# One matmul of every expert tile moved into the weights: b3 made part of the up weights, in a routed mixture-of-experts kernel

## What is computed

```python
x = x + conv_part(layernorm_c(x))          # attention over each image, ends in a product with Wr plus br
t = layernorm_t(x)                         # mean 0, variance 1 over the 128 channels of a token
logits = t @ Wg                            # 8 experts
top_logits, top_idx = top_k(logits, 2)     # two experts for each token
C = one_hot(top_idx) * softmax(top_logits)
h = t @ W1[e]                              # 128 -> 384
g = t @ W3[e] + b3[e]                      # 128 -> 384, with a bias
out = sum_e C[e] * (silu(h) * g) @ W2[e]   # 384 -> 128
x = x + out
```

## Time and profile before

| | |
|---|---|
| median of 3 runs | 313.33 us (312.4 to 313.88) |
| the profiled execution, its own time | 314.3 us |
| its span, first to last instruction | 312.6 us |
| TensorE matmul, busy | 257.9 us (83%) |
| VectorE, busy | 197.9 us (63%) |
| ScalarE, busy | 149.3 us (48%) |
| GpSimd, busy | 138.5 us (44%) |
| mean granted clock of TensorE | 0.927 |

### The profile page before, as it was taken

The page is one execution under the profiler, slowest core; times in us unless marked ns, Lnnn a source line. Parts: engine busy times, 40 slices in busy tenths (PEclk is TensorE's granted clock), DMA queues, the critical chain, the costliest instruction groups (busy, mean ns, idle before and its releaser), DMA issues.

```text
span 312.6 us, 6759 instructions
## 1 busy us (share of the span) xinstructions
PE 257.9 (83%) x1688; PEld 218.2 (70%) x1688; DVE 197.9 (63%) x812; ACT 149.3 (48%) x406; POOL 138.5 (44%) x151
## 2 busy tenths in 40 slices
PE   0899898977299999699998957989999999999200
PEld 0356564554289889598887946879999999999200
DVE  5554858888447765867566585776555555555742
ACT  1475474945365586376458326633443443443100
POOL 8000017666307626724772772577444344334500
PEclk9969969979579999999999999999999999999855
DMA  4799101111124201132210112323331221019187
GB/s 118 253 293 270 22 1 44 45 51 35 43 63 112 63 17 45 51 78 81 78 59 27 44 51 78 95 80 112 84 88 52 54 69 45 29 36 288 38 265 272
DMA packets 32248, 28.36 MB, mean 91 GB/s; under 512 B 5658, under 2 KB 30052, under 8 KB 32212
## 3 DMA queue, kind: packets, MB, share of 16 engines
q1 hardware_dynamic: 25120, 16.85, 19.5%
q0 software_dynamic: 4320, 8.92, 8.6%
q10 hardware_dynamic: 2772, 2.17, 2.1%
HBM read 15.89 MB, written 12.01 MB: 89 GB/s over the span
## 4 chain that ended last, share of the span: by engine, by line
PE 60%; DVE 18%; issue 8%; DMA 6%; POOL 4%; ACT 3%; SPq 1%; DVEq 0%; POOLq 0%; ACTq 0%
PE bank L674 13%; PE bank L664 7%; PE bank L645 7%; PE bank L646 6%; PE bank L647 6%; PE bank L633 5%; DMA both<-result_rows 3%; PE bank L649 3%; PE bank L640 2%; POOL sorted_rows L1383 2%; PE bank L600 2%; PE bank L563 2%; DVE stats L1029 2%; DVE act_rows L1261 1%; PE bank L591 1%
## 5 line engine op out<-in xcount | busy, mean ns | idle before, releaser
L1390 POOL DMA_INDIRECT result_rows<-ys,xs x71 | 69.2, 975 | 73.6 <-ACT ys L910 61.9
L1383 POOL DMA_INDIRECT sorted_rows<-row_buf,position x64 | 63.0, 984 | 82.4 <-ACT row_buf L867 43.7
L910 ACT ACTIVATE ys<-bank,xs 128x128 f32<-128x128 f32 x71 | 26.0, 367 | 84.0 <-PE bank L674 84.0
L674 PE MATMUL bank<-w_down,act_t 128*128 x426 | 59.6, 276 | 4.2 <-ACT ys L910 4.2
L674 PEld LDWEIGHTS bank<-w_down,act_t 128*128 128x128 f32 x426 | 53.1, 192 | 5.4 <-issue 5.4
L645 PE MATMUL bank<-w_up,xs_hi 128*128 x142 | 54.4, 383 | 0.0
L1261 DVE TENSOR_TENSOR act_rows<-both,bank 128x384 f32<-128x384 f32 x71 | 38.9, 548 | 18.4 <-PE bank L649 17.1
L1254 DVE TENSOR_TENSOR xs_lo<-bank,xs_hi 128x128 fp32r<-128x128 f32 x71 | 20.6, 290 | 46.6 <-ACT xs_hi L898 46.4
L646 PE MATMUL bank<-w_up,xs_lo 128*128 x142 | 48.2, 339 | 0.0
L647 PE MATMUL bank<-w_up,xs_hi 128*128 x142 | 48.0, 338 | 0.0
L664 PE MATMUL bank<-ident,act_rows 128*128 128x128 f32 x213 | 36.1, 279 | 10.0 <-DVE act_t L1267 9.3
...
## 6 DMA issues: line engine op xcount, KB each, us to landing
...
w_down<-L_ffn_W_dram SPq DMA_DIRECT2D x3, 512.0 KB, 10.3
...
result_rows<-ys,xs POOLq DMA_INDIRECT x71, 2.3
```

The source lines that it names most:

```text
L674: last = nc.tensor.matmul(bank[4][:, 0:C], act_t[s.par][:, k * P:(k + 1) * P], w_down[:, ds(e, 1), k * C:(k + 1) * C].rearrange("p a c -> ...
L1383: nc.gpsimd.indirect_dma_start(out=sorted_rows.ap(), out_offset=bass.IndirectOffsetOnAxis(ap=position[u.par][:, c:c + 1], axis=0), in_=row ...
L1390: nc.gpsimd.indirect_dma_start(out=result_rows.ap(), out_offset=bass.IndirectOffsetOnAxis(ap=xs[s.ring][:].bitcast(I32)[:, DEST:DEST + 1], ...
```

## The change

A normalised row sums to zero over its 128 channels. So the last row of an up weight matrix can be subtracted from every row without changing the product: then row 127 is zero, and what column 127 of the rows holds doesn't matter. The changed kernel writes 1.0 there once (`row_buf`, two memsets), lets `normalise_t` write 127 columns, and puts b3 in row 127 of the W3 matrix. `remake_up(e)` does this on TensorE: a product with `elim` (the identity less its last row in each row) for each of the two matrices, and a third matmul that adds b3's row, all in fp32 of 384 columns. The result is in PSUM (banks 4 and 5 for even experts, 6 and 7 for odd ones), from where `round_weights` and `split_up` now take it, in two operations of 384 columns each instead of one of 768. `up` loses the b3 matmul, and b3's parts, their 16 transfers and GpSimd's memset fall away.

An expert stands at two places of a step, `middle` and `end`, in steps -1 to 3. The `end` one is subtracted on TensorE as the last thing of the step; it is rounded and split in the next step. `split_up` runs at the end of VectorE's step for both, and `remake_up(e)` waits until expert e - 2 is split.

In the lead, VectorE's conversions go to step -1 (`convert_consts`, with `elim` and `b3_row`), statistics of a unit come earlier, ScalarE does several of its operations in another order, and no `keep_busy` is left in step -1; 14 stand in front, 7 in each of steps 0 to 3.

```diff
-            return {-1: (0,), 0: (1, 2), 1: (3, 4), 2: (5, 6, 7)}.get(i.n, ())
+            return {-1: (None, 0), 0: (1, 2), 1: (3, 4), 2: (5, 6), 3: (7, None)}.get(i.n, (None, None))
+        def up_banks(e):
+            return (bank[4], bank[5]) if e % 2 == 0 else (bank[6], bank[7])
...
-            sp.wait_ge(pool_steps, 2)
-            for part, done, half in ((b3_hi, b3_hi_ready, 0), (b3_lo, b3_lo_ready, 1)):
-                sp.wait_ge(done, 1)
-                for e in range(E):
-                    sp.dma_start(b3_parts[:].bitcast(F32)[half:half + 1, e, :], part[:].bitcast(F32)[e:e + 1, :]).then_inc(b3_ready, 16)
...
+            def remake_up(e):
+                pe.wait_ge(early_in if e < LOADED_FIRST else late_in, EXPERT_LOADS)
+                pe.wait_ge(elim_ready, 1)
+                pe.wait_ge(b3_in, 16)
+                at_least(pe, up_lo_ready, e - 1)
+                h, g = up_banks(e)
+                nc.tensor.matmul(h[:, 0:F], elim[:], w_raw[:, e, 0, :], start=True, stop=True)
+                nc.tensor.matmul(g[:, 0:F], elim[:], w_raw[:, e, 1, :], start=True, stop=False)
+                nc.tensor.matmul(g[:, 0:F], b3_row[:, e, :], b3_in8[:], start=False, stop=True).then_inc(up_ps, 1)
+            def keep_busy(n, o=bank[7]):
...
-                last = nc.tensor.matmul(o, xs_hi[s.par][:], w[1], start=False, stop=(j == 0))
-                if j == 1:
-                    last = nc.tensor.matmul(o, ones_row[:], b3_parts[:, ds(e, 1), :].rearrange("p a f -> p (a f)"),
-                                            start=False, stop=True)
-                last.then_inc((h_ps, g_ps)[j], 1)
+                nc.tensor.matmul(o, xs_hi[s.par][:], w[1], start=False, stop=True).then_inc((h_ps, g_ps)[j], 1)
...
-                    pe.wait_ge(b3_ready, 16 * 2 * E)
...
-                warm_up = -1 <= i.n < FIRST_STEP
+                warm_up = 0 <= i.n < FIRST_STEP
+                middle, end = experts_of_step(i)
...
-                if warm_up:
-                    keep_busy(4)
...
-                    keep_busy(3)
+                    at_least(pe, up_lo_ready, 2 * i.n)
+                    keep_busy(4)
...
-                if i.n == -2:
-                    logits_of_weights()
-                if i.n == -1:
-                    weights_product()
...
-                    keep_busy(6)
+                if middle is not None:
+                    remake_up(middle)
                 turn(slot_of_turn(i, 5))
                 if exists(later):
                     transpose_xn(later)
-                if warm_up:
-                    keep_busy(3)
+                if i.n == -1:
+                    weights_product()
...
-            pe.wait_ge(dve_consts, 2)
-            keep_busy(10)
+                if i.n == -2:
+                    logits_of_weights()
+                if end is not None:
+                    remake_up(end)
+            pe.wait_ge(dve_consts, 1)
+            keep_busy(14)
...
-                        row_buf[u.par][:, t, :, 0:C],
-                        x1_all[:, ds(u.n * TPU + t, 1), :].broadcast_to([P, K, C]),
+                        row_buf[u.par][:, t, :, 0:C - 1],
+                        x1_all[:, ds(u.n * TPU + t, 1), 0:C - 1].broadcast_to([P, K, C - 1]),
...
-                act.wait_ge(early_in if e < LOADED_FIRST else late_in, EXPERT_LOADS)
-                nc.scalar.activation(w_up[:, e, :, 0, :], w_raw[:, e], ACT.Copy).then_inc(up_hi_ready, 1)
-            def round_b3():
-                act.wait_ge(b3_in, 16)
-                nc.scalar.activation(b3_hi[:], b3_in8[:], ACT.Copy).then_inc(b3_hi_ready, 1)
+                act.wait_ge(up_ps, e + 1)
+                for j in range(2):
+                    last = nc.scalar.activation(w_up[:, e, j, 0, :], up_banks(e)[j][:, 0:F], ACT.Copy)
+                last.then_inc(up_hi_ready, 1)
...
-            dve.wait_ge(pool_consts, POOL_CONSTS)
-            nc.vector.tensor_copy(iota_e[:], iota_ei[:])
-            nc.vector.tensor_copy(region[:], region_i[:])
-            nc.vector.tensor_copy(ring_up[:], ring_upi[:])
-            nc.vector.tensor_copy(slot_ids[:], slot_ids_i[:]).then_inc(dve_consts, 1)
+            nc.vector.memset(mean_of, 1.0 / C).then_inc(dve_consts, 1)
             dve.wait_ge(dve_consts, 2)
             nc.vector.memset(two_ones[0:2, :], 1.0).then_inc(dve_consts, 1)
-            nc.vector.tensor_tensor(up_to[:], iota_e[0:1, :].unsqueeze(1).broadcast_to([1, E, E]),
-                                    iota_e[0:1, :].unsqueeze(2).broadcast_to([1, E, E]), ALU.is_le)
+            def convert_consts():
+                dve.wait_ge(pool_consts, POOL_CONSTS)
+                nc.vector.tensor_copy(iota_e[:], iota_ei[:])
+                nc.vector.tensor_copy(region[:], region_i[:])
+                nc.vector.tensor_copy(ring_up[:], ring_upi[:])
+                nc.vector.tensor_copy(slot_ids[:], slot_ids_i[:])
+                nc.vector.memset(row_buf[0][:, :, :, C - 1], 1.0)
+                nc.vector.memset(row_buf[1][:, :, :, C - 1], 1.0)
+                nc.vector.tensor_scalar(elim[:], ident[:], ident[:, P - 1:P], None, ALU.subtract)
+                nc.vector.memset(b3_row[:], 0.0).then_inc(dve_consts, 1)
+                dve.wait_ge(dve_consts, 4)
+                nc.vector.tensor_copy(b3_row[:, :, P - 1], ident[0:E, 0:E]).then_inc(elim_ready, 1)
+                nc.vector.tensor_tensor(up_to[:], iota_e[0:1, :].unsqueeze(1).broadcast_to([1, E, E]),
+                                        iota_e[0:1, :].unsqueeze(2).broadcast_to([1, E, E]), ALU.is_le)
...
-                nc.vector.tensor_tensor(w_up[:, e, :, 1, :], w_raw[:, e],
-                                        w_up[:].bitcast(F32)[:, e, :, 0, :], ALU.subtract).then_inc(up_lo_ready, 1)
-            def split_b3():
-                dve.wait_ge(b3_hi_ready, 1)
-                nc.vector.tensor_tensor(b3_lo[:], b3_in8[:], b3_hi[:].bitcast(F32),
-                                        ALU.subtract).then_inc(b3_lo_ready, 1)
+                for j in range(2):
+                    last = nc.vector.tensor_tensor(w_up[:, e, j, 1, :], up_banks(e)[j][:, 0:F],
+                                                   w_up[:].bitcast(F32)[:, e, j, 0, :], ALU.subtract)
+                last.then_inc(up_lo_ready, 1)
...
+                    stats_of_x(i.shift(3))
+                    add_eps(i.shift(3))
                 turn(slot_of_turn(i, 2))
                 if exists(new):
                     invert_sums(new)
+                if i.n == -1:
+                    convert_consts()
+                    split_br()
...
-                    split_up(e)
...
-                for e in weights:
-                    if e != weights[0]:
+                for e in (before, middle):
+                    if e is not None:
...
-            nc.gpsimd.memset(b3_parts[:].bitcast(F32), 0.0).then_inc(pool_steps, 1)
```

76 lines of the change are left out of this document (36 added, 40 removed).

## The result

| | before | after |
|---|---|---|
| median, both run side by side | 314.09 us (19 runs, 312.03 to 318.15, and one of 435.41) | 310.5 us (19 runs, 307.7 to 318.76) |
| the profiled execution, its own time | 314.3 us | 310.68 us |
| its span | 312.6 us | 308.9 us |
| mean granted clock of TensorE | 0.927 | 0.919 |

The ratio is 0.9878, with a 95% interval of 0.9849 to 0.9907: the change makes the kernel faster, by some 3.8 us where 10.3 were forecast. 310.5 us also lies outside the range.

A forecast was written before the change was run, and what follows sets the result against it. TensorE was taken to bound the last stretch, the middle in part, with the start a chain of its own; -5.8 - 3.7 - 0.8 = -10.3 us gave a 303.0 us median, own range 301 to 306, wider range 298.5 to 308.5.

The forecast's parts named there:

- The last stretch: 205 to 290 us, bound by TensorE: the b3 matmul's 6.8% of 85 us all comes back, 5.8 us.
- The start of the statistics: Lead: first statistics at 3.5 to 4 us and ScalarE's first logarithm at 5.7, 3.4 us earlier.
- The place of the new wait: Steps 1 and 2: TensorE's subtraction waits after each `member` for VectorE's split of weights, 1.0 us.
- The term kept as 0: Lead: delay of TensorE's first subtraction if the conversions' 2.59 us are their own; taken as 0, with 0.8 us kept.
- I take 3.7: Middle, 86 to 205 us: the b3 matmul's 3.1% of 119 us comes back, 3.7 us.
- the bound of 0: Middle, 86 to 205 us: the least the removed b3 matmul could give back, nothing; the other bound was 7.0 us.
- rival 2: The middle doesn't follow: VectorE's gating and act_t and ScalarE take line 649's place; -6.6, 306.7 us, chance 0.17.
- the start, -0.8 forecast: Up to the first tile: -5.0 + 0.2 + 1.15 = -3.6 us at the high clock, +2.8 for a low stretch.
- These come out about even: Lead: fewer warming matmuls (4.1 us) balance the added constants and subtraction, so 3.4 us carries to the transposes, 22.5 us.
- my bounds, 2.0 and 3.4: Steps before the scatter: the subtraction's three fp32 matmuls of 384 columns take 2.0 to 3.4 us; 2.0 taken.
- 2.8 for the clock: Start: one long stretch of TensorE's low clock expected again in the steps, +2.8 us.
- rival 3: The start loses: low clock in every step or subtraction at its upper bound; -4.7, 308.6 us, chance 0.08.

The follow-up runs named there:

- experiment 1: The kernel before with its fourth g matmul, the one adding b3, left out and nothing else changed: 308.02 us, ratio 0.9769 to the kernel before.
- experiment 2: The kernel after with a matmul put back in each tile's g, a row of ones times the weights' rest: 317.91 us, ratio 1.0086 to the kernel before.
- experiment 6: The kernel after without the `xs_lo` product for g: 302.0 us; also with act_t copied by 128 of 384 columns in tiles 2 to 37: 303.13 us.
- experiment 7: The kernel after with five warming matmuls ahead of `weights_product`: 307.75 us, ratio 0.9824; also with the subtraction moved behind the weighing: 308.9 us, median of ten.
- experiment 5: The kernel after with act_t copied by 128 of 384 columns in tiles 2 to 37: 306.55 us; with a g matmul put back too: 315.29 us.

## Why the prediction was wrong

**Right.** The last stretch: -5.80 us for -5.8, with the reasoning that TensorE's chain there is unbroken. The row with the one cost nothing. The start of the statistics (3.94) and of the logarithm (5.68). The place of the new wait. The four conversions, moved behind the second unit's work, took 0.15 to 0.18 us each, with GpSimd idle (0.00 us busy from 9 to 24 us), so the 2.59 us of the earlier trace rows were waiting for GpSimd's memset. The Trainium skill (SBUF — State Buffer, "Who interferes with whom") says that a cast in VectorE's two-port mode and a GpSimd operation can't share the ports: whoever issues first holds them for its whole instruction and the other is blocked. Both traces agree: the memset began at 4.47, the casts at 4.57. The term kept as 0 was 0.

**The failed step: "I take 3.7"** for the middle. It read the b3 line's 3.1% share of the chain as time that comes back. Over the whole middle nothing came back (experiments 1, 2 and 6). From tile 1 to tile 22, at the high clock, it was 0.9 us of the 2.1 that 3.7 us gives to 21 of 37 distances: of the 2.9 us that TensorE was busy less, it waited 1.7 longer for VectorE's copy. The line was on the chain because the chain follows whoever was last at each turn, and the others were close behind. The sum had no term for low stretches of the clock behind tile 22, nor for the 0.91 us of tile 0 to 1. The evidence for the bound of 0 was in the reading itself, 'VectorE lines and "issue" take more', and should have decided: where several engines alternate on the chain, a line's share is an upper bound. The rows to ask were the waits of that stretch and not of the whole page: the 17.1 us of the earlier trace rows belong to the last stretch, and in the middle the transposes already waited 8.2 us for act_t and `xs_lo` some 26 us for ScalarE (88 to 207 us). This was rival 2, to which I gave 0.17. Its middle came out in number, and its mechanism in part.

**The second failed step: the start, -0.8 forecast, +2.0 measured.** First tile's rows are transposed at 88.04 where my steps, all at the high clock, gave 86.06 - 3.6 = 82.46: 5.6 us, in these pieces.
- The lead to the transposes of probabilities: 24.26 for 22.5, +1.8. "These come out about even" was the choice without a row. The reordered lead makes TensorE wait 2.31 us, and its clock was low for 13.7 us; with both changed in experiment 7 they came at 21.27. The same lead gave 22.61 to 24.56 in other executions, so this piece goes from 0.1 to 2.1 us between executions.
- From there to mix 29.50 - 24.26 = 5.2 for 3.8 us, +1.4, at the low clock for 3.0 us of it; then to the end of `member` 6.9 for 6.4, +0.5.
- Two steps took 14.42 and 14.11 us for 13.5 each, +1.5. At the high clock: three products 2.37 us for 2.0 (nearer the lower of my bounds, 2.0 and 3.4), the split with its hand-over 37.47 - 36.39 = 1.08 for 1.0, transposes to mix 4.2 for 4.0, and the rest in what follows mix.
- `member` to scatter 64.92 to 73.91: 9.0 for 8.6, +0.4, with the clock low from 70.1 us on.

Against 5.6 I had set 2.8 for the clock, and put it in the steps, where it was high. It fell in the lead instead, which I had taken from the kernel before, with 6.8 us of low clock in it. Since the low clock was a single amount added to the sum, it could not be checked part by part. The sum of the start is also known less well than +2.0 sounds: the start of the kernel before gave 90.33 and 87.24 us (experiment 1), that of the kernel after 90.63 to 93.62.

**The range.** Rivals 2 and 3 were kept as alternatives; both came true at once, rival 3 in part. -5.8 + 0 + 2.0 = -3.8 lies outside a range that reached only to one of them. The two do not depend on each other, and the upper end should have held their sum.

**Open.** Whether the removal itself brings the low clock behind tile 22. Each of the ten profiled executions without the matmul has it, for 3.4 to 10.3 us between 160 and 205 us, behind waits for act_t and for ScalarE's `ys` (0.54 and 0.98 us in the kernel after, 2.27 us in the row below); of the three with it, before and experiment 2 have none, and experiment 5 with the matmul has 3.4 us. Less work for TensorE means longer waits for act_t, and so it may be the cause. But three executions are few, and the kernel before waited 1.68 and 2.14 us for act_t at 182 and 187 us without falling. Warming matmuls in that wait were not tried. A row of it, from the profiled execution with the steps at the high clock (the same matmul of line 657 takes 0.34 us at 182.17 and 0.52 us at 188.16):

```profile
184.78 0.55 PE L670 MATMUL bank<-ident,act_rows 128*128 128x128 f32 x3 [2.27 <-DVE act_t L1277]
```
